# Spreading weight chunks, z rows and value tiles' loads, with identity products ahead of the first tile and the edge keys at a later tile

## The chip, the cores and the metric

The kernel runs on one core of one Trainium2 chip. The metric is the device time of one execution in microseconds (us), the median of several runs. A core has TensorE (PE, matrix products), VectorE (DVE), ScalarE (ACT), GpSimd (POOL) and SyncE (SP, which here only issues transfers); each works through its own instruction list in order, and semaphores order the engines among each other. Transfers between device memory and the on-chip buffer are issued by SP, ACT and POOL and carried by 16 DMA engines.

## What is computed

The reference is one layer on 2500 nodes with 1024 features: layer norm, a graph aggregation, an attention-like mix whose result is the value projection, and a feed-forward with ternary weights and rounded activations.

```python
xn = layernorm(x)
gnn = segment_sum((xn @ W)[src] * edge_w[:, None], dst, 2500)   # 42500 edges
q, k, v = xn @ Wq.T + bq, xn @ Wk.T + bk, xn @ Wv.T + bv
q, k = q / norm(q), k / norm(k)          # norms over the whole array
s = sum(phi(q) * phi(k), over the map)   # phi: exp of a product with mix weights
x = x + gnn + s * v / s
y = layernorm(x)
x = x + bitlinear(silu(bitlinear(y, w_gate)) * bitlinear(y, w_up), w_down)
```

`bitlinear` rounds each row of the input to 8-bit integers and the weights to -1, 0, 1.

## The kernel before, in words

The nodes are 20 tiles of 125 rows (`TILES`, `ROWS`), handled in 10 pairs (`HALF`), the two of a pair in buffers 0 and 1. In each product of single-precision data both factors are split into a high and a low part, and three matmuls give the product (`product3`, lines 374 to 376). ACT makes the high part, DVE subtracts it to get the low part, so each operand passes ACT, then DVE, then PE.

**First Gram pass** (PE lines 1522 to 1552). For each tile n: DVE computes row statistics (`row_sums`) and normalises (`normalise`, signals `s_xn`); PE turns the tile by eight transposes (line 1530); ACT copies the high part into a ring of three slots (`high_of_rows`), DVE the low part (`low_of_rows`, `s_lo`), and PE adds the tile's Gram products (lines 1515 to 1517, `s_gm`). ACT also brings the transposed tile out of PSUM and writes it to memory (`transposed_rows`, `write_transposed`; four buffers). At tile 4 PE transposes the edge keys and edge weights (line 1545), ACT copies them (line 808) and writes them as rows to memory (line 812, `s_kout`); at tile 5 the bias rows follow. The keys are computed by DVE in `edge_keys`, called ahead of tile 4, from two index ramps that POOL writes with `iota` (line 693) right after the identity. POOL then copies the identity to bf16, clears `zeros`, and writes zeros over the dense edge matrices in strips, strip r after 4r tiles.

**Second Gram pass and maps.** From tile 20 on, DVE does one pair of edge columns (`edges`) after each low part; that needs the key rows, broadcast to all partitions by SP (`load_key_rows`, issued after `s_kout`, ahead of the loads of `raw`). The pairs are then scattered into the two dense matrices by POOL until about 941 us.

**Value stage ("stage 4").** The matrix WH/WL holds the value weights in columns turned block by block (`high_of_block`, `low_of_block`, `s_vl`). For each tile PE multiplies, DVE adds the bias and scales (`stage4_tile`, `s_z`), SP loads x, stores the sum as z and loads the next transposed tile (`load_tile`) in the order of its list: for pair h and buffer i, load of tile t + 2, then z's store, then the wait for that store, then x's load. ACT's `high_of_tile` waits for the load and for PE to be done with the buffer.

**Aggregation.** Five groups of four target tiles (`GROUPS`, `GT`); for each group all 20 source tiles are multiplied, m = g * 10 + h counting the pairs. SP loads blocks of the two dense matrices (`load_next_A`, lines 601 to 605), DVE adds the two (`sum_of_blocks`, line 1282), ACT and DVE split the block (AH, AL) and the source (SH, SL; `SH_first`, `SL_first` for m = 0), and PE adds the products into eight PSUM banks (`sources`). PE's signal `s_pe5[i]` lets ACT overwrite buffer i. The first group waits for the last z tile before its target tile 1 (`s_z[1]`). At a group's end DVE adds z (`zr`, `add_z`) and later normalises and rounds the rows. For group 0, SP loads all of `zr` (2 MB) after A's load 1.

**Chunks.** During group 0 the three feed-forward matrices are made ternary in 12 chunks of 128 rows: POOL loads a chunk (`load_chunk`, chunks 0 and 1 after both first `s_pe5`), DVE scales and rounds it (two steps), ACT copies it to bf16, DVE turns its blocks, POOL writes it in eight transfers (`store_halves`). `CHUNKS_AT` says how many fall to each pair: 0, 0, 1, 1, 2, 1, 2, 1, 2, 2. SP loads them back as `wT` in three parts at A's loads 12, 13 and 14.

## Time and profile before

| | us |
|---|---|
| three runs, median | 1673.24 |
| three runs, lowest and highest | 1671.74, 1677.58 |
| the profiled execution | 1673.33 |
| its span, first to last instruction | 1671.3 |
| PE busy | 1638.4 |
| DVE, ACT, POOL busy | 1115.9, 495.5, 640.8 |

The span is the profiled execution's own time without what lies around it, here 2.0 us. A row of a timeline begins with the start in us from the span's start and the duration in us, and an entry in brackets tells how long the engine had been idle before and what it was released by. The mean granted clock of PE is 0.999 of full speed.

### The profile page before, as it was taken

The page shows a single profiled execution, that of the slowest core. Times are in us where ns is not written, and L with a number is a line of the kernel's source. Part 1 is how long each engine was busy: PE and PEld are TensorE (multiplying, and loading weights), DVE is VectorE, ACT ScalarE, POOL GpSimd, SP SyncE. Part 2 cuts the span into 40 slices and gives each one's busy share as a digit, 9 for nine tenths or more (in the row PEclk, how much of TensorE's full clock was granted, in tenths as well). Part 3 has the DMA queues.
Part 4 walks back from the last instruction along what each step waited for, and adds up shares of the span by engine and source line. Part 5 has one row for each costly group of instructions (what it writes and reads, how often), then busy time and mean ns, then how long its engine had stood idle before and what let it go on. Part 6 is the DMA issues. An engine that isn't in the chain of part 4 may idle for free.

```text
span 1671.3 us, 22573 instructions
## 1 busy us (share of the span) xinstructions
PE 1638.4 (98%) x7876; PEld 1328.2 (79%) x7876; DVE 1115.9 (67%) x2568; ACT 495.5 (30%) x598; POOL 640.8 (38%) x497
## 2 busy tenths in 40 slices
PE   6999999999999999999999999999999999999998
PEld 5999999877777888887888877878877877787665
DVE  7876583667777766655555566787575674674886
ACT  4632311322111111122300024433333332332553
POOL 2011555777777777776688405620000000000000
PEclk9999999999999999999999999999999999999999
DMA  9999978665686665557866556655445345433554
GB/s 312 397 406 338 312 247 251 170 150 112 167 207 146 180 150 146 131 135 177 239 131 141 140 178 197 194 174 161 122 137 138 110 129 135 135 113 96 148 172 123
DMA packets 154688, 302.87 MB, mean 181 GB/s; under 512 B 61537, under 2 KB 92305, under 8 KB 154626
## 3 DMA queue, kind: packets, MB, share of 16 engines
q1 hardware_dynamic: 78382, 206.81, 39.5%
q0 software_dynamic: 66192, 62.07, 16.8%
q10 hardware_dynamic: 10052, 33.26, 6.5%
q8 instruction: 27, 0.44, 0.1%
q14 instruction: 35, 0.29, 0.1%
HBM read 202.88 MB, written 99.20 MB: 181 GB/s over the span
## 4 chain that ended last, share of the span: by engine, by line
PE 84%; DVE 8%; DMA 4%; issue 2%; ACT 1%; POOL 0%; SPq 0%; ACTq 0%; DVEq 0%
PE PS L374 21%; PE PS L375 21%; PE PS L376 21%; PE PS L1515 4%; PE PS L1517 4%; PE PS L1516 4%; PE PS L1749 4%; DMA Aside<-A_dense 3%; PE PS L1779 2%; PE PS L1579 2%; DVE stats L1316 1%; DVE SL L1289 1%; DVE zr L1310 1%; DVE AL L1291 1%; DVE stats L1053 1%
## 5 line engine op out<-in xcount | busy, mean ns | idle before, releaser
L721 POOL DMA_INDIRECT A_dense<-wtot,cell x333 | 537.9, 1615 | 219.5 <-DMA A_dense<-wtot,cell 125.0
L374 PE MATMUL PS<-SL,AH 125*125 125x512 f32 x784 | 308.4, 393 | 6.7 <-DVE AL L1291 6.2
L375 PE MATMUL PS<-SH,AL 125*125 125x512 f32 x784 | 309.6, 395 | 0.0
L376 PE MATMUL PS<-SH,AH 125*125 125x512 f32 x784 | 309.4, 395 | 0.0
L374 PE MATMUL PS<-WL,xtH 128*125 128x512 f32 x640 | 251.9, 394 | 3.2 <-DVE xtL L1178 3.2
L375 PE MATMUL PS<-WH,xtL 128*125 128x512 f32 x640 | 251.6, 393 | 0.0
L376 PE MATMUL PS<-WH,xtH 128*125 128x512 f32 x640 | 251.2, 393 | 0.0
L1289 DVE TENSOR_TENSOR SL<-S,SH 125x1024 fp32r<-125x1024 f32 x98 | 119.5, 1220 | 136.5 <-ACT SH L944 136.5
L944 ACT ACTIVATE SH<-S 125x1024 fp32r<-125x1024 f32 (+1 forms) x98 | 103.9, 1061 | 334.0 <-PE PS L376 334.0
L374 PEld LDWEIGHTS PS<-SL,AH 125*125 125x125 f32 x784 | 145.4, 185 | 47.2 <-DVE AL L1291 9.2
L375 PEld LDWEIGHTS PS<-SH,AL 125*125 125x125 f32 x784 | 145.7, 186 | 36.2
L376 PEld LDWEIGHTS PS<-SH,AH 125*125 125x125 f32 x784 | 145.1, 185 | 35.0
L386 DVE SCALAR_TENSOR_TENSOR junk<-keyrow,key,ewrow 128x256 bf16<-128x256 f32 x336 | 148.8, 480 | 1.2 <-DMA ewrow<-weight_rows 1.2
L374 PEld LDWEIGHTS PS<-WL,xtH 128*125 128x125 f32 x640 | 118.5, 185 | 33.1 <-DVE xtL L1178 4.1
L376 PEld LDWEIGHTS PS<-WH,xtH 128*125 128x125 f32 x640 | 118.6, 185 | 29.2
L375 PEld LDWEIGHTS PS<-WH,xtL 128*125 128x125 f32 x640 | 118.7, 185 | 28.8
L375 PE MATMUL PS<-TH,xtL 128*125 128x512 f32 x320 | 126.5, 395 | 0.0
L376 PE MATMUL PS<-TH,xtH 128*125 128x512 f32 x320 | 126.0, 394 | 0.0
L374 PE MATMUL PS<-TL,xtH 128*125 128x512 f32 x320 | 125.9, 393 | 0.0
L1178 DVE TENSOR_TENSOR xtL<-xt,xtH 128x1000 fp32r<-128x1000 f32 x60 | 71.5, 1191 | 78.7 <-ACT xtH L862 75.2
L862 ACT ACTIVATE xtH<-xt 128x1000 fp32r<-128x1000 f32 x60 | 62.0, 1033 | 188.9 <-DMA xt<-xnT 188.3
L705 POOL DMA_DIRECT2D A_dense<-zeros x40 | 46.1, 1153 | 139.9 <-PE PS L1517 78.4
(190 smaller groups left out, 2602.3 us busy)
## 6 DMA issues: line engine op xcount, KB each, us to landing
A_dense<-zeros POOLq DMA_DIRECT2D x40, 1280.0 KB
xt<-xnT SPq DMA_DIRECT2D x60, 500.0 KB
Araw<-A_dense SPq DMA_DIRECT2D x100, 250.0 KB, 2.7
Aside<-A_dense SPq DMA_DIRECT2D x100, 250.0 KB, 3.0
keyrow<-key_rows SPq DMA_DIRECT2D x42, 512.0 KB
ewrow<-weight_rows SPq DMA_DIRECT2D x42, 512.0 KB
xnT<-XT ACTq DMA_DIRECT2D x20, 500.0 KB, 9.7
zx<-in_x SPq DMA_DIRECT2D x20, 448.0 KB
```

What stands on the lines that cost most here:

```text
L374: nc.tensor.matmul(o, lh, rl, start=start, stop=False)
L375: nc.tensor.matmul(o, ll, rh, start=False, stop=False)
L376: return nc.tensor.matmul(o, lh, rh, start=False, stop=stop)
L386: nc.vector.scalar_tensor_tensor(junk[:, slot, 2 * c:2 * c + 2, :].rearrange("p a n -> p (a n)"), row, key[:, col], wrow, ALU.is_equal, AL ...
L721: pool.indirect_dma_start(cells[m], bass.IndirectOffsetOnAxis(cell[:, col:col + 1], 0), wtot[:, col:col + 1], None, compute_op=ALU.add).th ...
L944: nc.scalar.activation(sh, S[0:ROWS, bass.ds(s, 1), :].rearrange("p o n -> p (o n)"), ACT.Copy).then_inc(s_s[i], 1)
L1178: nc.vector.tensor_tensor(xtL[i][:, :, :], xt[:, i], xtH[i][:, :, :].bitcast(F32), ALU.subtract).then_inc(s_xtl[i], 1)
L1289: nc.vector.tensor_tensor(sl, S[0:ROWS, bass.ds(s, 1), :].rearrange("p o n -> p (o n)"), sh.bitcast(F32), ALU.subtract)
L1515: nc.tensor.matmul(o, hi[:, cols], rl, start=first and opens, stop=False, skip_group_check=True)
L1516: nc.tensor.matmul(o, lo[:, cols], rh, start=False, stop=False, skip_group_check=True)
L1517: last = nc.tensor.matmul(o, hi[:, cols], rh, start=False, stop=last_one, skip_group_check=True)
L1749: last = nc.tensor.matmul(PS[0:ROWS, 2 * i + c, :], rqT[:, i, k, 0:ROWS], up_blocks(c, k), start=k == 0, stop=k == KT - 1)
```

## The change

Six things change; none of them alters what is computed.

- Ahead of its first tile PE multiplies the identity by itself ten times (`WARM`), into a bank that is written anew later.
- POOL writes the two index ramps after the first zero strip, when tile 1 is normalised, and no longer right after the identity; the first zero strip waits for tile 0's normalisation.
- DVE's `edge_keys` moves from ahead of tile 4 to ahead of tile 12's statistics (after tiles 10 and 11 are normalised), and the keys' and biases' transposes and copies from tiles 4 and 5 to tiles 14 and 15 (`KEYS_TILE`).
- SP issues the loads of value tiles 2 and 3 right after the last value block's load.
- One chunk per pair: chunks 0 to 8 in pairs 1 to 9 of group 0, chunks 9 to 11 in pairs 7 to 9 of group 1, which is therefore written out and no longer part of the loop. z's rows are loaded by tile after A's loads 2 to 5, and the three parts of `wT` after A's loads 12, 15 and 23.
- In PE's first pair of the aggregation both sources are multiplied for three target tiles, then the wait for the last z tile follows, then the fourth target tile for both.

The diff, cut to its core:

```diff
+KEYS_TILE = 14
+WARM = 10
...
-CHUNKS_AT = (0, 0, 1, 1, 2, 1, 2, 1, 2, 2)
+CHUNK_OF = {(0, h): h - 1 for h in range(1, HALF)} | {(1, h): h + 2 for h in range(3 + GT, HALF)}
+WEIGHTS_AT = (HALF + 2, HALF + 5, 2 * HALF + 3)
...
         sp.wait_ge(s_vl, 2)
         load_v_rows(7)
+        for i in range(2):
+            sp.wait_ge(s_xth[i], 2 * HALF + 1)
+            sp.wait_ge(s_xtl[i], 2 * HALF + 1)
+            load_tile(2 + i, i)
...
-            if not isinstance(h, int) or t + 2 < TILES:
+            if 0 < h < HALF - 1:
                 load_tile(nxt, i)
-            elif i:
+            elif h and i:
                 load_next_A(0)
...
         wait_stage4(sp)
-        load_next_A(1)
-        split_rows(sp, zr[:, :, :], z_d[0:GN, :].rearrange("(t r) d -> r t d", r=ROWS), s_zin)
-        for hh in range(2, HALF + 2):
+        for hh in range(1, WEIGHTS_AT[-1] + 1):
             load_next_A(hh)
-        for f in range(3):
-            for i in range(2):
-                sp.wait_ge(s_fout[i], 128 * (2 * f + 2))
-            sp.dma_start(wT[:, f], wT_d[4 * f:4 * f + 4].rearrange("c p n -> p c n")).then_inc(s_wT, 16)
-            load_next_A(HALF + 2 + f)
-        with sp.Fori(HALF + 5, GROUPS * HALF - 1) as hh:
+            if 2 <= hh < 2 + GT:
+                d = hh - 2
+                split_rows(sp, zr[:, d, :], z_d[d * ROWS:(d + 1) * ROWS, :], s_zin)
+            if hh in WEIGHTS_AT:
+                f = WEIGHTS_AT.index(hh)
+                for i in range(2):
+                    sp.wait_ge(s_fout[i], 128 * (2 * f + 2))
+                sp.dma_start(wT[:, f], wT_d[4 * f:4 * f + 4].rearrange("c p n -> p c n")).then_inc(s_wT, 16)
+        with sp.Fori(WEIGHTS_AT[-1] + 1, GROUPS * HALF - 1) as hh:
             load_next_A(hh)
...
-        for t in (key, away):
-            pool.iota(t[:, :], [[0, ROWS_C // 2], [1, 2]], base=A_PITCH - 2, channel_multiplier=A_PITCH,
-                      allow_small_or_imprecise_dtypes=True).then_inc(s_fill, 1)
...
         pool.wait_ge(s_const, 8)
-        for r in range(STRIPS):
-            if r:
-                pool.wait_ge(s_gm, min(4 * r, TILES))
+        pool.wait_ge(s_xn, 1)
+        zero_strip(0, 0)
+        pool.wait_ge(s_xn, 2)
+        for t in (key, away):
+            pool.iota(t[:, :], [[0, ROWS_C // 2], [1, 2]], base=A_PITCH - 2, channel_multiplier=A_PITCH,
+                      allow_small_or_imprecise_dtypes=True).then_inc(s_fill, 1)
+        for r in range(1, STRIPS):
+            pool.wait_ge(s_gm, min(4 * r, TILES))
             zero_strip(0, r)
...
-            if n == 4:
+            if n == KEYS_TILE:
                 for q in range(2):
                     act.wait_ge(s_tr0, q + 2)
...
+        def high_beside_chunk(g, h):
+            high_of_pair(g, h)
+            if (g, h) in CHUNK_OF:
+                c = CHUNK_OF[g, h]
                 act.wait_ge(s_fr[c % 2], c // 2 + 1)
                 if c >= 2:
                     act.wait_ge(s_fT[c % 2], c // 2)
                 nc.scalar.activation(gqb[:, c % 2, :], gwb[:, c % 2, :], ACT.Identity, bias=neg_round[:, :]).then_inc(s_fq16[c % 2], 1)
...
             if a == 2:
                 low_of_rows(2)
+            if a == KEYS_TILE - 4:
                 edge_keys()
...
-            dve.wait_ge(s_zin, g * 32 + 32)
+            dve.wait_ge(s_zin, 32 * GT + g * 32)
...
+        def low_beside_chunk(g, h):
+            m = g * HALF + h
+            c = CHUNK_OF[g, h]
+            i, f = c % 2, c // 4
+            low_of_sources(2 * h, 0, m)
+            sum_of_blocks(1, m)
+            dve.wait_ge(s_gw[i], c // 2 * 16 + 16)
+            nc.vector.tensor_scalar(gwb[:, i, :], gwb[:, i, :], wq_sc[:, f:f + 1, 1], 1.0,
+                                    ALU.mult, ALU.min).then_inc(s_fm, 1)
+            dve.wait_ge(s_fm, c + 1)
+            nc.vector.tensor_scalar(gwb[:, i, :], gwb[:, i, :], -1.0, ROUND, ALU.max, ALU.add).then_inc(s_fr[i], 1)
+            low_of_sources(2 * h + 1, 1, m)
+            sum_of_blocks(0, m + 1)
+            dve.wait_ge(s_fq16[i], c // 2 + 1)
+            if c >= 2:
+                dve.wait_ge(s_fout[i], c // 2 * 128)
+            turn_blocks(gTb[:, i, :], gqb[:, i, :]).then_inc(s_fT[i], 1)
+
         for h in range(1, HALF):
...
+            low_beside_chunk(0, h)
...
+        group(1)
+        for h in range(3 + GT - 1, HALF):
+            if (1, h) in CHUNK_OF:
+                low_beside_chunk(1, h)
+            else:
+                low_of_pair(1, h)
+        with dve.Fori(2, GROUPS - 1) as g:
             group(g)
...
         pe.wait_ge(s_const, 6)
+        for n in range(WARM):
+            nc.tensor.matmul(PS[:, 0, 0:P], ident[:, :], ident[:, :], start=True, stop=True)
         pe.wait_ge(s_pad, 3)
...
-            if n == 4:
-                pe.wait_ge(s_xev[0], 3)
+            if n == KEYS_TILE:
+                pe.wait_ge(s_xev[0], n // 2 + 1)
...
-                    if d == 1:
-                        pe.wait_ge(s_z[1], HALF)
...
+        def first_sources(i, tiles):
+            sh, sl = (b[0:ROWS, :] for b in first_S[i])
+            for d in tiles:
+                rows = slice(d * ROWS, (d + 1) * ROWS)
+                for c in range(2):
+                    cols = slice(c * 512, (c + 1) * 512)
+                    last = product3(PS[0:ROWS, 2 * d + c, :], AH[i][0:ROWS, rows], AL[i][0:ROWS, rows],
+                                    sh[:, cols], sl[:, cols], i == 0, False)
+            return last
+
+        for i in range(2):
+            pe.wait_ge(s_lo5[i], 1)
+            first_sources(i, ORDER[:-1])
+        pe.wait_ge(s_z[1], HALF)
+        for i in range(2):
+            first_sources(i, ORDER[-1:]).then_inc(s_pe5[i], 1)
+        other_sources(0)
```

## Rows read from the trace of the kernel before

**Rows 1.** The page's first part: busy time, share of the span, instructions.
```profile
PE 1638.4 (98%) x7876; PEld 1328.2 (79%) x7876; DVE 1115.9 (67%) x2568; ACT 495.5 (30%) x598; POOL 640.8 (38%) x497
```

**Rows 2.** PE's waits over the span: us in total, times, longest us.
```profile
PE PS L374 <- DVE AL L1291: 6.2, 6, 2.1
...
PE PS L374 <- DVE xtL L1178: 3.2, 2, 2.4
...
PE PS L374 <- DVE zr L1310: 0.5, 1, 0.5
```

**Rows 3.** Timeline of the start, four engines: start us, duration us, instruction.
```profile
5.22 1.93 POOL L693 IOTA away<- 128x336 f32 x1
...
6.98 1.44 DVE L1065 TENSOR_SCALAR X<-X,mv,rstd 125x1024 f32<-125x1024 f32 x1
...
7.35 0.51 POOL L697 MEMSET zeros<- 128x512 f32 x1
...
8.68 1.90 PE L1530 MATMUL PS<-ident,X 125*128 125x125 f32 x8 [8.68 <-DVE X L1065]
...
11.05 0.81 DVE L1065 TENSOR_SCALAR X<-X,mv,rstd 125x1024 f32<-125x1024 f32 x1
...
14.71 1.02 PE L1530 MATMUL PS<-ident,X 125*128 125x125 f32 x8
...
17.47 1.53 DVE L1065 TENSOR_SCALAR X<-X,mv,rstd 125x1024 f32<-125x1024 f32 x2
...
20.55 0.50 DVE L1076 SCALAR_TENSOR_TENSOR key<-iedge 128x332 f32<-128x332 int32 x1
```

**Rows 4.** Key rows: ACT's issue, packets at 46 to 48 us, DVE's first edge pair.
```profile
35.22 0.58 ACTq L812 DMA_DIRECT2D key_rows<-kT_sb  x1
...
DMA packets 284, 0.74 MB, mean 368 GB/s; under 512 B 27, under 2 KB 111, under 8 KB 284
...
83.43 0.48 DVE L386 SCALAR_TENSOR_TENSOR junk<-keyrow,key,ewrow 128x256 bf16<-128x256 f32 x1
...
86.44 1.23 DVE L1070 TENSOR_TENSOR ring<-X,ring 125x1024 fp32r<-125x1024 f32 x1 [1.43 <-ACT ring L772]
```

**Rows 5.** Timeline of the value stage's first tiles, SP and DVE.
```profile
763.27 0.34 SPq L539 DMA_DIRECT2D xt<-xnT  x1
...
782.09 0.35 SPq L539 DMA_DIRECT2D xt<-xnT  x1
...
788.61 1.20 DVE L1178 TENSOR_TENSOR xtL<-xt,xtH 128x1000 fp32r<-128x1000 f32 x1 [7.69 <-ACT xtH L862]
```

**Rows 6.** Beginning of aggregation: timelines of PE, ACT, POOL; landing of chunk loads.
```profile
983.73 0.47 PE L374 MATMUL PS<-SL_first,AH 125*125 125x512 f32 x1 [1.01 <-DVE zx L1251]
...
985.47 1.06 ACT L944 ACTIVATE SH<-S 125x1024 fp32r<-125x1024 f32 x1 [9.33 <-PE PS L376]
...
990.99 1.06 ACT L944 ACTIVATE SH<-S 125x1024 fp32r<-125x1024 f32 x1 [3.95 <-PE PS L376]
...
991.61 1.19 POOL L743 DMA_DIRECT2D gwb<-in_L_ffn_w_gate  x2 [50.82 <-PE PS L376]
...
gwb<-in_L_ffn_w_gate POOLq DMA_DIRECT2D x2, 512.0 KB, 4.4
```

**Rows 7.** DVE's timeline; PE's waits in 990:1020, 1080:1100, 1120:1140, 1220:1240 us.
```profile
1011.66 0.68 DVE L1282 TENSOR_TENSOR Araw<-Araw,Aside 125x500 f32<-125x500 f32 x1 [6.66 <-DMA Aside<-A_dense]
...
PE PS L374 <- DVE AL L1291: 2.1, 1, 2.1
...
1086.27 0.75 DVE L1367 TENSOR_SCALAR gwb<-gwb,wq_sc 128x1024 f32<-128x1024 f32 x1 [4.55 <-DMA gwb<-in_L_ffn_w_down]
...
PE PS L374 <- DVE AL L1291: 1.7, 1, 1.7
...
PE PS L374 <- DVE AL L1291: 1.2, 1, 1.2
...
PE PS L374 <- DVE AL L1291: 0.3, 1, 0.3
```

More of the change, by code:

```diff
@@ L96 @@
 END_AT = 229368
-CHUNKS_AT = (0, 0, 1, 1, 2, 1, 2, 1, 2, 2)
-assert len(CHUNKS_AT) == HALF and sum(CHUNKS_AT) == 12
+CHUNK_OF = {(0, h): h - 1 for h in range(1, HALF)} | {(1, h): h + 2 for h in range(3 + GT, HALF)}
+assert sorted(CHUNK_OF.values()) == list(range(12))
+WEIGHTS_AT = (HALF + 2, HALF + 5, 2 * HALF + 3)
 def split_rows(eng, dst, src, sem):
@@ L966, in _ @@
         act.wait_ge(s_mm[1], 3 * HALF)
-        chunk = 0
-        for h in range(1, HALF):
-            high_of_pair(0, h)
-            for c in range(chunk, chunk + CHUNKS_AT[h]):
+        def high_beside_chunk(g, h):
+            high_of_pair(g, h)
+            if (g, h) in CHUNK_OF:
+                c = CHUNK_OF[g, h]
                 act.wait_ge(s_fr[c % 2], c // 2 + 1)
@@ L974, in _, with high_of_group @@
                 nc.scalar.activation(gqb[:, c % 2, :], gwb[:, c % 2, :], ACT.Identity, bias=neg_round[:, :]).then_inc(s_fq16[c % 2], 1)
-            chunk += CHUNKS_AT[h]
+        for h in range(1, HALF):
+            high_beside_chunk(0, h)
         def move_rows(g):
             return bass.ds(g * GN, GN)
-        with act.Fori(1, GROUPS) as g:
+        def high_of_group(g):
             high_of_pair(g, 0)
@@ L993, in _ @@
             split_rows(act, zr[:, :, :], z_d[move_rows(g), :].rearrange("(t r) d -> r t d", r=ROWS), s_zin)
+        high_of_group(1)
+        for h in range(3 + GT, HALF):
+            high_beside_chunk(1, h)
+        with act.Fori(2, GROUPS) as g:
+            high_of_group(g)
             with act.Fori(3 + GT, HALF) as h:
@@ L1685, in sources @@
             sh, sl = SH[0:ROWS, i, :], SL[0:ROWS, i, :]
-            if isinstance(m, int) and m == 0:
-                sh, sl = (b[0:ROWS, :] for b in first_S[i])
             for d in ORDER:
```

33 lines of the change are left out of this document (7 added, 26 removed).

## Prediction

> **What bounds the kernel now.** The first page says that TensorE (PE) is busy 98% of the span [rows 1], so a change can only win PE's few idle microseconds: 1671.3 less 1638.4 is 33, of which 8.7 lie ahead of the first transpose [rows 1, 3]; the rest is PE's waits and the tail behind its last product. I therefore read the list of PE's waits first, then the timeline around each. In the reader's eye it should fall into places: the start, where PE follows VectorE (DVE) tile by tile; one 2.4 us wait in the value stage, for the tile split at 788.61 [rows 2, 5]; 1.01 us where aggregation begins [rows 6]; and 2.1, 1.7 + 0.5 and 1.2 us in the first and second group of aggregation [rows 2, 7]. Between about 87 and 776 us PE has no wait at all, so what is won at the start is kept.
>
> **Start: constants and first tile.** In the kernel before, the copy to bf16 and the zero strip's memset stand behind two iotas of 1.95 us on GpSimd (POOL) and so run while DVE normalises tile 0, which takes 1.44 us; the next one takes 0.81 [rows 3]. With the iotas gone from there, both POOL steps end near 4.2 us and tile 0 takes 0.81: -0.63, on the path, since DVE is the engine that all others follow here. The iotas (3.9 us) now start when tile 1 is normalised, 11.05 + 0.81 = 11.9, less 0.6, and end near 15.2; the next normalisation starts at 17.47 less 0.6 [rows 3], so they don't meet, and the keys wait for them only much later. The Trainium skill, page "SBUF — State Buffer", section "Who interferes with whom", says that a VectorE instruction in its two-port mode and a GpSimd instruction exclude each other for the whole instruction, whichever began first; if the iota did overlap the normalisation, that rule would give back up to 1.9 us, and the rows leave 1.6 us between them.
>
> **Ten products of the identity.** They fit between 3.4 us (the identity is ready) and 7.8; bound from the rows: eight cold transposes take 1.90 [rows 3], so ten products of like shape some 2.4 us, at most twice that if a plain product costs double, still done by 8.2. No semaphore waits on them. They can only save time by letting tile 0 run with short matmuls (1.02 for eight transposes against 1.90). But PE then waits longer for DVE: its next work, tile 2, is normalised at 17.47 + 0.81 whatever PE does, and PE is done with tile 1 at 18.2 even now. Cost and gain: 0.
>
> **Edge keys from tile 2 to tile 10, their transposes from tile 4 to 14.** DVE loses 1.02 us (20.55 to 21.57) ahead of tile 4 and gets it back ahead of tile 10. In steady state DVE spends about as long for a pair of tiles as PE, so the key step shows as a new PE wait of 1.0 at tile 10. ScalarE's (ACT) copies, two DMA issues (the first 0.58, [rows 4]) and the bias rows' turn stall PE at tile 15 as they did at tile 5. I walked the three queues through all 20 tiles with the rows' durations and these semaphores: before, the last tile's Gram products end at 86.3 as in the trace; after, at 85.6. So the stage gives -0.65, the 0.63 of tile 0; bounds 0 (lead used up by slower landings) and -1.7 (the key step hidden at tile 10).
>
> What moves with it is SP's queue: the broadcast loads of the key rows wait for the key writes, and DVE's first edge pair (at 83.43 now) for them. Today the key writes are issued at 35.22 and their small packets are seen until about 47 [rows 4], i.e. 11 us. After, ACT issues near 71.5 to 72.5; the input tiles are loaded by then, so I take 7 us for landing, then 7 us for the first megabyte of rows: 86. An edge pair of 1.6 us must be over 1.15 us plus a little before PE needs the next split tile, which today is begun at 86.44 with 1.43 us of waiting before it and needed at 90.3 [rows 4]: the rows may be as late as 87. Cost 0, bounds 0 and +4 (11 us and 8 us instead).
>
> **Value tiles' loads.** Today SP loads tile 2 at 763.27 and tile 3 only at 782.09, behind the store of tile 0 [rows 5]; the latter makes PE wait 2.4. Both now go right after the eighth value block's load, at about 751 and 757. ACT's split of tile 2 still waits for PE to leave the buffer, so PE's 0.8 us ahead of tile 2 (xtL waits, 3.2 in all [rows 2]) stays; tile 3's split is ready by 782.2, before PE needs it at 787.4. Tile 4's load stays behind the store of tile 1 and was 1.8 us ahead of need, less than the 2.4 won; without tile 3's half megabyte in the queue the store lands earlier. -2.2, bounds -1.8 and -2.4.
>
> **First sources, three tiles of each, then the fourth.** The wait of 1.01 for the last z tile [rows 6] goes: PE has 36 products x 0.23 = 8.4 us to do first. But the buffer of source 0 is now released after both: 24 products take 5.54 (985.47 to 990.99, ACT's two starts, [rows 6]); from 978.5, both sources end at 989.7 and the first is released at 988.6 instead of 985.5. Three steps hang on this (SH on ACT, SL and AL on DVE, 3.0 us), so the next source is ready at 991.65: a new wait of 1.95.
>
> **One chunk per pair, from the first pair.** DVE now waits for chunk 0 in pair 1, between the splits of two sources. POOL still loads it only when both first sources are done: issue 991.61 today, 0.9 earlier after, landing 4.4 [rows 6], so 995.1 to 995.3. Then two steps of 0.7, SL 1.14, AL 0.6: 998.6, and PE is free at 991.65 + 5.57 = 997.2. A second new wait, 1.35, bounds 0 and +3. Queued behind that wait on DVE: the split of source 3, the next block sum and chunk 0's turn. So the beginning of aggregation costs 1.95 + 1.35 - 1.01 = +2.3.
>
> **z rows by tile, and chunks 9 to 11 in group 1.** The 2 MB of z went ahead of the next A blocks, and DVE waited 6.66 for one: PE 2.1 [rows 7]. Half a megabyte after each of four pairs has 5 us until the next A load: -2.05. Two chunks in the last pair made DVE wait 4.55 at 1086.27 and PE 1.7, then 0.5 for the sums of z [rows 2, 7]; with one chunk per 11.1 us pair both go: -2.2. In group 1 the wait of 1.2 falls to what the later groups show with no weights in the queue, 0.3 [rows 7]: the first weights' load now comes behind the A blocks. -0.85; bounds for the three -3.5 and -5.3.
>
> **Sum.** -0.65 + 0 + 0 - 2.2 + 2.3 - 2.05 - 2.2 - 0.85 = -5.65. Against the profiled execution, 1673.33, that is 1667.7; its time is within 0.1 of the median of the runs, 1673.24, from which 1667.6 follows. I write 1667.6.
>
> **Rivals.** (a) *The key rows come too late and PE stalls in the second Gram pass*: slower than before. For it: the DMA engines are fully busy there, the landing took 11 us in the rows. Against it: SP's queue holds nothing else at that time. PE loses each microsecond beyond 87; the sum is used up at a landing of 92.7, and at 98 the kernel is 5 slower, 1678. (b) *Chunk 0 or the released buffer costs more*, its load sharing the queues with A blocks: at the bound +3 instead of 1.35, and z's rows in the way once more by 1: 1670.3. (c) *The identity products pay*: The Trainium skill, page "TensorE: Matmul & The Clock Gate", Part 1, says the clock is full only for an engine that has been busy, which speaks for this. As a mechanism here: tile 0's 8 transposes and six slow products are over some 2.4 us earlier and this reaches the end: 1665.2. Against it, PE's wait for tile 2. (d) *The spreading doesn't do what it says*: A's wait at 1011.66 comes from something else (the ternary stores or the chunks), 2.05 stays: 1669.7.
>
> **Chances.** Forecast 0.55, (a) 0.12, most of it a stall of 1 to 4 us, only 0.05 as large as to end slower; (b) 0.15; (c) 0.08; (d) 0.10. About 0.3%, 5.0 us, is what a measurement of this kernel can tell from no change. Faster by more (below 1668.2): most of the forecast's case (0.47) and (c), 0.55. Within: the rest of it, (b), (d), most of (a), 0.40. Slower: 0.05. The unknown costs alone reach from 1664.0 (-1.7 at the start, chunk 0 in time) to 1672; the range is 1663.5 to 1672.5.
>
> **What would show it.** First normalisation 0.81, last first-pass product near 85.6; a wait of 1 us at tile 10; first edge pair near 86 with no PE wait behind it; no xtL wait near 787; two new AL waits, about 1.9 and 1.4, near 985; none of 2 us near 1007; none above 0.5 in the second group. A PE wait behind the first edge pairs, or more than 4 us in the first two pairs of aggregation, makes the prediction wrong.

## The result, and the profile after

The changed kernel takes 1668.48 us (median of 9 runs, 1666.82 to 1669.69); the kernel before took 1674.46 beside it (9 runs). The ratio is 0.9958, 95% interval 0.9948 to 0.9967: 0.42% faster, where 0.34% was forecast. The medians themselves differ by 6.0 us, the ratio stands for 7.0. The ratios of this document leave out a single run of 5816 us, of the kernel with the old order of PE's first sources. The profiled execution's span fell from 1671.3 to 1666.6 us.

The page's busy times, the answer to [rows 1], and then PE's waits over the span (us in total, times, longest us), the answer to [rows 2]:

```profile
PE 1643.1 (99%) x7896; PEld 1333.1 (80%) x7896; DVE 1115.9 (67%) x2568; ACT 487.1 (29%) x591; POOL 636.8 (38%) x497
...
PE PS L1543 <- DVE ring L1090: 5.5, 4, 2.3
PE PS L1552 <- POOL earlier L698: 3.4, 1, 3.4
PE PS L377 <- DVE AL L1312: 3.4, 6, 1.7
...
PE PS L377 <- DVE xtL L1199: 0.8, 1, 0.8
```

The waits for AL fell from 6.2 to 3.4 us and those for xtL from 3.2 to 0.8. PE's busy time rose by 4.7 us, most of it by 20 more matmuls (the ten products of the identity show as 20, 4.35 us together); further down there are also two stretches in which products run at half clock.

The start, answering [rows 3], from the timelines of PE, DVE and SP (start us, duration us, instruction, idle time before it):

```profile
3.38 4.35 PE L1552 MATMUL PS<-ident 128*128 128x128 f32 x20 [3.38 <-POOL earlier L698]
...
6.67 0.81 DVE L1085 TENSOR_SCALAR X<-X,mv,rstd 125x1024 f32<-125x1024 f32 x1
...
7.59 1.05 PE L1560 MATMUL PS<-ident,X 125*128 125x125 f32 x8
...
8.38 7.34 SPq L501 DMA_DIRECT2D brows<-in_L_mix_bq  x1
...
27.07 2.47 DVE L1073 BATCH_NORM_STATS2 stats<-X 125x6 f32<-125x512 f32 x4 [1.68 <-DMA X<-in_x]
...
31.01 0.65 PE L1543 MATMUL PS<-ring 125*128 125x512 f32 x1 [2.35 <-DVE ring L1090]
31.45 0.63 PE L1544 MATMUL PS<-ring 125*128 125x512 f32 x1
...
87.30 0.28 PE L1543 MATMUL PS<-ring 125*128 125x258 f32 x1
```

Tile 0 is normalised in 0.81 us, as forecast, and turned at full clock. But DVE then waits 1.68 us for pair 3 of x, PE 2.35 us at tile 4, and behind that wait nine products start 0.32 to 0.43 us apart instead of 0.17 to 0.23. The first product of 258 columns, my mark for "15 tiles done" (called the 258-column product from here on), stands at 87.30 against 86.48 before: the start is 0.82 us slower, not 0.65 faster. What follows can be told by a ledger. ACT's high part of a source (line 954, 98 times) is released by PE at the same place in both kernels, so the difference of its n-th starts, after less before, is how far PE is ahead:

| place | before | after | difference | step | forecast |
|---|---|---|---|---|---|
| 15 tiles done | 86.48 | 87.30 | +0.82 | +0.82 | -0.65 |
| value stage, its last product on PE | 978.14 | 976.62 | -1.52 | -2.34 | -2.2 |
| aggregation, 4th start | 1002.10 | 1002.94 | +0.84 | +2.36 | +2.3 |
| 7th start | 1021.10 | 1019.62 | -1.48 | -2.32 | -2.05 |
| 21st start | 1101.74 | 1097.51 | -4.23 | -2.75 | -2.2 |
| 39th start (about the end of group 1) | 1203.39 | 1198.85 | -4.54 | -0.31 | -0.85 |
| 98th start | 1533.94 | 1529.39 | -4.55 | 0 | 0 |

The first two places are starts on PE. The value stage's step is the 2.43 us wait that is gone; the row of the list above shows its one wait left, 0.8. The begin of aggregation, answering [rows 6], timelines of ACT, POOL, PE and DVE:

```profile
986.89 1.06 ACT L954 ACTIVATE SH<-S 125x1024 fp32r<-125x1024 f32 x1 [12.27 <-PE PS L379]
...
988.85 1.19 POOL L753 DMA_DIRECT2D gwb<-in_L_ffn_w_gate  x2 [53.67 <-PE PS L379]
...
989.93 0.50 PE L377 MATMUL PS<-SL,AH 125*125 125x512 f32 x1 [1.74 <-DVE AL L1312]
...
990.61 0.63 PE L379 MATMUL PS<-SH,AH 125*125 125x512 f32 x1
...
992.72 0.75 DVE L1389 TENSOR_SCALAR gwb<-gwb,wq_sc 128x1024 f32<-128x1024 f32 x1 [2.26 <-DMA gwb<-in_L_ffn_w_gate]
```

The wait for z is gone and 1.74 us for the late buffer is new, both as forecast. Behind it PE runs at half clock until about 993.7. DVE waits 2.26 us for chunk 0, but PE, slowed down, never feels it. And late in group 1, DVE (answering [rows 7]):

```profile
1172.44 0.68 DVE L1303 TENSOR_TENSOR Araw<-Araw,Aside 125x500 f32<-125x500 f32 x1 [4.84 <-DMA Aside<-A_dense]
1173.04 0.75 DVE L1389 TENSOR_SCALAR gwb<-gwb,wq_sc 128x1024 f32<-128x1024 f32 x1
1173.82 0.69 DVE L1392 TENSOR_SCALAR gwb<-gwb 128x1024 f32<-128x1024 f32 x1
1174.43 1.22 DVE L1310 TENSOR_TENSOR SL<-S,SH 125x1024 fp32r<-125x1024 f32 x1
1175.57 0.67 DVE L1312 TENSOR_TENSOR AL<-Araw,AH 125x500 fp32r<-125x500 f32 x1
```

An A block that came late, two steps of a chunk behind it, and only then the source's low part: PE waits 0.5 us here, at a place where before had no wait. Yet before had the same late block. ACT loads 2 MB of z rows in this group, in one piece, at 1164.75 us before and at 1159.20 after, and the A block issued 3 us behind it takes 9.7 us to land before and 9.9 after, where the blocks ahead of it took about 3. DVE before:

```profile
1177.99 0.68 DVE L1282 TENSOR_TENSOR Araw<-Araw,Aside 125x500 f32<-125x500 f32 x1 [4.83 <-DMA Aside<-A_dense]
1178.58 1.22 DVE L1289 TENSOR_TENSOR SL<-S,SH 125x1024 fp32r<-125x1024 f32 x1
```

There the low part stands right behind the late sum; the 1.4 us of chunk 9's two steps between them are what is new.

### The profile page after: what moved, and what is told of

It is laid out like the page before. It is cut to its first block, busy times and chain, and to the rows that moved or that the text cites. A ratio compares the mean times of both kernels' runs of the same rounds, so it can differ in the third digit from the quotient of the medians.

```text
span 1666.6 us, 22401 instructions
## 1 busy us (share of the span) xinstructions
PE 1643.1 (99%) x7896; PEld 1333.1 (80%) x7896; DVE 1115.9 (67%) x2568; ACT 487.1 (29%) x591; POOL 636.8 (38%) x497
## 4 chain that ended last, share of the span: by engine, by line
PE 85%; DVE 7%; DMA 5%; SPq 1%; issue 1%; ACT 1%; DVEq 0%; ACTq 0%
PE PS L377 21%; PE PS L378 21%; PE PS L379 21%; PE PS L1543 5%; PE PS L1545 5%; PE PS L1544 5%; PE PS L1794 4%; DMA Aside<-A_dense 3%; PE PS L1824 2%; PE PS L1609 2%; DVE SL L1310 1%; DVE stats L1337 1%; DVE zr L1331 1%; DVE AL L1312 1%; DMA z<-zx 1%
```

## The experiments

Twelve kernels, in three series of four. Each ratio is against before, from runs on the same chip; an interval reaches 0.12 to 0.22 points to each side, which is 2 to 4 us, so the profiles carry the finer readings. Each kernel has one profiled execution.

**Without the identity products.**

```diff
-WARM = 10
+WARM = 0
```

> The changed kernel without the ten products of the identity; all else stays. Theory (the products pay nothing, because the first tile's transposes are followed by waits for tiles 1 to 3 either way): time within 0.3 us of the changed kernel; tile 0's transposes take 1.9 us instead of 1.05, and the wait that follows is shorter by the same 0.85, so that tile 1's transposes start at the same offset; the half-clock products of 31 to 34.5 us stay. Rival (the identity products pay, since they bring full clock to the first tiles): slower by 1 to 2.5 us, with later transposes of tiles 1 to 3 and a first pass that ends later by as much.

Ratio 0.9960 (0.9948 to 0.9973), against 0.9958 with them: no cost and no gain in time. Its trace, PE:

```profile
8.28 1.90 PE L1560 MATMUL PS<-ident,X 125*128 125x125 f32 x8 [8.28 <-DVE X L1085]
10.61 0.80 PE L1543 MATMUL PS<-ring 125*128 125x512 f32 x1 [0.42 <-DVE ring L1090]
...
30.54 0.50 PE L1543 MATMUL PS<-ring 125*128 125x512 f32 x1 [1.58 <-DVE ring L1090]
```

The transposes take 1.90, as in [rows 3], the first eight products behind them are slow, and the 30.54 product is at full clock: the half-clock stretch has gone back to tile 0, where DVE is waited for anyway. My theory that the stretch behind tile 4 would stay was wrong; that the products gain nothing was right. The 258-column product comes at 86.04. DVE's wait for pair 3 is 0.92 here, though nothing was changed for it. Near 988 this kernel has the same wait of 1.74 us as the changed one, but no slow products behind it; there 0.36 us for chunk 0 shows instead.

**The bias rows' loads behind pair 4's.**

```diff
-        for i, v in enumerate((bq, bk)):
-            sp.dma_start(brows[0:KT, i, :], ...)
         for p in range(3, NP):
             sp.wait_ge(s_st, 2 * (p - 2))
             load_pair(p)
+            if p == 4:
+                for i, v in enumerate((bq, bk)):
+                    sp.dma_start(brows[0:KT, i, :], ...)
```

> The changed kernel with the two loads of the bias rows issued on SP behind the load of pair 4 of x, not ahead of pair 3's. In the changed kernel SP spent 7.34 us on them (8.38 to 15.7), pair 3's load was issued at 16.42, DVE waited 1.68 us for it, PE waited 2.35 us at tile 4 (31.01) and its products ran at half clock until about 34.5. Theory (the late pair 3 is what ate the start's gain): no wait of DVE for pair 3, none over 0.5 us of PE near 31, no products of 0.63 us there, and a first pass that ends 1.5 to 3.5 us earlier: faster than the changed kernel by that. Rival (the wait near 31 comes from the DVE's own order of work, not from the load): pair 3 lands earlier, PE's wait stays over 1.5 us, time within 0.5 us of the changed kernel.

Ratio 0.9961 (0.9947 to 0.9975). DVE's wait for pair 3 and PE's at tile 4 are gone, as the theory said; yet a half-clock stretch is there all the same, now from about 20.4 us, and the 258-column product comes at 86.33: 0.97 us earlier than in the changed kernel, not 1.5 to 3.5. The long issue only moved: SP needs 3.76 and 2.70 us for pair 3's two transfers in place of 7.34 for the bias rows.

**The old order of PE's first sources.**

```diff
-        for i in range(2):
-            pe.wait_ge(s_lo5[i], 1)
-            first_sources(i, ORDER[:-1])
-        pe.wait_ge(s_z[1], HALF)
-        for i in range(2):
-            first_sources(i, ORDER[-1:]).then_inc(s_pe5[i], 1)
+        pe.wait_ge(s_lo5[0], 1)
+        first_sources(0, ORDER[:-1])
+        pe.wait_ge(s_z[1], HALF)
+        first_sources(0, ORDER[-1:]).then_inc(s_pe5[0], 1)
+        pe.wait_ge(s_lo5[1], 1)
+        first_sources(1, ORDER).then_inc(s_pe5[1], 1)
```

> The changed kernel with the old order of TensorE's first products of the aggregation: all four tiles of source 0, a wait for the last z tile ahead of its tile 1, then all of source 1. Theory (moving that wait behind source 1 made source 0's buffer free later, so DVE's SL and AL of the next pair are late by the 1.74 us wait near 990): PE waits about 1.0 us for z near 986, the 1.74 us wait near 990 goes, and the products of 0.63 us that followed it (990 to 993.4, some 1.6 us lost) go too, unless chunk 0, whose wait of DVE is now bare, brings a PE wait of 1 to 2.4 us at the next source. Sum between -2.3 and +0.8 us against the changed kernel. Rival (chunk 0, not the buffer, makes that wait): the 1.74 us wait stays and 1.0 us is added.

Ratio 0.9969 (0.9956 to 0.9982): 1.8 us above the changed kernel by the ratios, with intervals that overlap; I had expected -2.3 to +0.8. PE and DVE:

```profile
981.93 0.49 PE L377 MATMUL PS<-SL_first,AH 125*125 125x512 f32 x1 [0.93 <-DVE zx L1272]
...
993.67 0.76 DVE L1389 TENSOR_SCALAR gwb<-gwb,wq_sc 128x1024 f32<-128x1024 f32 x1 [6.42 <-DMA gwb<-in_L_ffn_w_gate]
...
996.94 0.50 PE L377 MATMUL PS<-SL,AH 125*125 125x512 f32 x1 [2.26 <-DVE AL L1312]
```

The 1.74 us wait is gone: it did come from the late buffer. The z wait is back, 0.93, and chunk 0, no longer covered, costs 2.26. So the forecast's two new waits are two mechanisms, and this kernel shows the second without the first. At ACT's 4th start it is 0.1 us ahead of the changed kernel; it falls behind in group 1, where it waits 2.26 us near 1178 and the changed one 0.5.

**New order: one tile of source 1 ahead of the z wait, source 3's low part ahead of chunk 0.**

```diff
         pe.wait_ge(s_lo5[0], 1)
         first_sources(0, ORDER[:-1])
+        pe.wait_ge(s_lo5[1], 1)
+        first_sources(1, ORDER[:1])
         pe.wait_ge(s_z[1], HALF)
         first_sources(0, ORDER[-1:]).then_inc(s_pe5[0], 1)
+        first_sources(1, ORDER[1:]).then_inc(s_pe5[1], 1)
...
+            if m == 1:
+                low_of_sources(2 * h + 1, 1, m)
+                sum_of_blocks(0, m + 1)
             dve.wait_ge(s_gw[i], c // 2 * 16 + 16)
...
-            low_of_sources(2 * h + 1, 1, m)
-            sum_of_blocks(0, m + 1)
+            if m != 1:
+                low_of_sources(2 * h + 1, 1, m)
+                sum_of_blocks(0, m + 1)
```

> The changed kernel with two edits at the start of the aggregation: TensorE does source 0's tiles 0, 2, 3, then source 1's tile 0, then waits for z, does source 0's tile 1 and frees its buffer, and then source 1's tiles 2, 3, 1; and DVE does the low part and the sum of source 3 before the steps of chunk 0. Theory (the 1.74 us wait near 990 comes from the late release of source 0's buffer, and the slow products behind it from that wait): source 0 is freed 1.9 us or more earlier, neither the 1.01 us z wait nor the 1.74 us wait is there, no products over 0.6 us between 985 and 1000, and chunk 0's load is covered: 2.0 to 3.3 us faster than the changed kernel. Rival (the slow products belong to the time or the load on the chip and not to the wait): the products of 0.63 us stay, and only 1.2 to 1.7 us is gained.

Ratio 0.9940 (0.9921 to 0.9960), 1665.29 us. The stretch 990:1000 (busy us and instructions of PE, PEld, DVE, ACT, POOL, then granted clock, DMA share, GB/s) of the changed kernel and then of this one:

```profile
990.00:1000.00 10.00, 10.00 (x37) 7.88 (x38) 6.91 (x9) 3.35 (x4) 2.61 (x6) 0.83 0.75 244
```

```profile
980.00:990.00 10.00, 10.00 (x45) 7.99 (x44) 6.25 (x7) 2.13 (x3) 0.00 (x0) 1.00 0.22 59
990.00:1000.00 10.00, 10.00 (x45) 8.01 (x44) 7.14 (x9) 3.62 (x5) 3.47 (x7) 1.00 0.74 248
```

"Busy" is 10.00 in all of them, and only the counts and the clock tell that the first did 37 products and the others 45. From the value stage's last product to ACT's 4th start this kernel takes 22.7 us, the changed one 26.3 and before 24.0: 3.6 us are gained at this place. The profile's gain (1664.3 against 1666.6) is smaller, mainly by the 1.38 us that PE waits at 800.62 for a load of the value stage.

**The identity products alone, in the kernel before.**

```diff
         pe.wait_ge(s_const, 6)
+        for n in range(10):
+            nc.tensor.matmul(PS[:, 0, 0:P], ident[:, :], ident[:, :], start=True, stop=True)
         pe.wait_ge(s_pad, 3)
```

> The kernel before with the ten products of the identity ahead of tile 0, and nothing else of the change. In the looks so far each of the four kernels with these products had its cold stretch (products of 0.63 us, some 3.5 us long) between 20 and 35 us, and the two without had it at tile 0 (11 to 13.5 us), where 1.3 us waits for DVE follow anyway. Theory (the products only move the cold stretch from covered to bare work): tile 0's products at full clock, a stretch of 0.63 us products between 18 and 36 us, and the first product of 258 columns between 86.5 and 88.5 us against 86.48 of before: 0 to 2 us slower. Rival (they pay, as in the third rival of the forecast): no stretch behind tile 0 and the first product of 258 columns 0.5 to 1.5 us earlier than before's. Rival (they do nothing either way): within 0.3 us of 86.48.

Ratio 1.0006 (0.9993 to 1.0019). PE:

```profile
11.00 0.50 PE L1515 MATMUL PS<-ring 125*128 125x512 f32 x1 [1.43 <-DVE ring L1070]
...
20.70 0.79 PE L1515 MATMUL PS<-ring 125*128 125x512 f32 x1 [1.28 <-DVE ring L1070]
21.29 0.63 PE L1516 MATMUL PS<-ring 125*128 125x512 f32 x1
...
32.45 0.51 PE L1515 MATMUL PS<-ring 125*128 125x512 f32 x1 [2.10 <-DVE ring L1070]
```

The slow stretch is where the theory put it, and the 258-column product is at 88.87, outside the 86.5 to 88.5 expected and 2.39 us later than before's; 1.5 us of that stand already at tile 4 (32.45 against 30.92), where a late pair 3 makes PE wait 2.10, so the products' own share is not told. By time it is no change. The rival in which the products pay falls: the interval leaves them 1.2 us at most, where it had 2.4.

**The value tiles' loads alone, in the kernel before.**

```diff
         load_v_rows(7)
+        for i in range(2):
+            sp.wait_ge(s_xth[i], 2 * HALF + 1)
+            sp.wait_ge(s_xtl[i], 2 * HALF + 1)
+            load_tile(2 + i, i)
...
-            if not isinstance(h, int) or t + 2 < TILES:
+            if 0 < h < HALF - 1:
                 load_tile(nxt, i)
-            elif i:
+            elif h and i:
```

> The kernel before with the value tiles' loads of tiles 2 and 3 issued ahead of the loop, one tile later for the rest, and nothing else of the change. Theory (the 2.43 us wait near 790 is for a load behind stores and x loads in SP's queue): that wait goes, no other over 0.5 us comes in the value stage but one at tile 1 of 0.80, and the kernel is 2.0 to 2.5 us faster than before. Rival (the wait is given back at the z wait or later in the stage): a new wait between 795 and 985 us and less than 1 us of gain. Since one look at a variant of the changed kernel had 1.38 us at 800 for the same kind of load, a wait of that size may show here too: then the gain is about 1 us.

Ratio 0.9982 (0.9967 to 0.9997): 3.0 us, interval 0.5 to 5.5, forecast 2.2. In the value stage only the 0.80 us wait is left, and from the 258-column product to the stage's last one 2.7 us are saved. Its trace teaches something else: at 1015 us, where before waits 2.05, and at 1089, where it waits 1.71, this kernel, with the same code there, waits 0 and 1.0. Its span of 1665.7 is thus 5.6 below before's, of which the edit gave 2.7; and this execution, at 1667.72, was the fastest of the twelve, whose median is 1672.86.

**z rows in one piece.**

```diff
         for hh in range(1, WEIGHTS_AT[-1] + 1):
             load_next_A(hh)
-            if 2 <= hh < 2 + GT:
-                d = hh - 2
-                split_rows(sp, zr[:, d, :], z_d[d * ROWS:(d + 1) * ROWS, :], s_zin)
+            if hh == 1:
+                split_rows(sp, zr[:, :, :], z_d[0:GN, :]...., s_zin)
...
-            dve.wait_ge(s_zin, 32 * GT + g * 32)
+            dve.wait_ge(s_zin, 32 + g * 32)
```

> The changed kernel with the z rows of group 0 loaded in one piece behind the first of the A loads, as before, and nothing else. Theory (z rows spread give 2.05 us): a PE wait of 1.5 to 2.5 us comes back between 1000 and 1025 us, and the kernel is 1.5 to 2.5 us slower than the changed one. Rival (the wait near 1015 was from two chunks falling on one pair, not from the z rows): no wait over 0.5 us there, time within 0.5 us of the changed kernel.

Ratio 0.9997 (0.9983 to 1.0011), against 0.9958: 6.5 us slower than the changed kernel, three times the forecast's term. The trace has the same: from ACT's 4th to 7th start 23.24 us, and 16.68 in the changed kernel. DVE and PE:

```profile
1012.84 0.68 DVE L1302 TENSOR_TENSOR Araw<-Araw,Aside 125x500 f32<-125x500 f32 x1 [7.65 <-DMA Aside<-A_dense]
1013.43 1.24 DVE L419 STREAM_TRANSPOSE gTb<-gqb 128x1024 bf16<-128x1024 bf16 x1
...
1016.42 0.79 PE L377 MATMUL PS<-SL,AH 125*125 125x512 f32 x1 [3.61 <-DVE AL L1311]
```

The mechanism is the forecast's (2 MB ahead of an A block, [rows 7]), but the chunks now begin in pair 1, so a chunk's turn stands between the late block and the split; PE waits 3.61 and then runs at half clock (233 products in 1000:1060 instead of 261). Spreading z is what makes early chunks affordable. Group 1, whose z rows still come in one piece, pays the same way at chunk 9.

**Three cures together: new order, no identity products, bias rows later.**

```diff
-WARM = 10
+WARM = 0
...
(the new order and the bias rows' loads as above)
```

> The changed kernel without the ten identity products, with the bias rows' loads behind pair 4's, and with the start of the aggregation as in the run with the new order (source 1's first tile ahead of the z wait, source 3's low part ahead of chunk 0). Theory (the three stalls are independent): first product of 258 columns at 84.5 to 85.6 us, no half-clock products but at tile 0, no PE wait between 980 and 1060, span 1660 to 1662.5 us, 0.55 to 0.7% faster than before. Rival (the starts are bounded by the loads of x and by DVE, so that two cures give what one gives): first product of 258 columns at 85.8 to 86.4 us and a span of 1662.5 to 1664.

Ratio 0.9937 (0.9915 to 0.9958), 1665.63 us, but a span of 1665.8, above what either case gave; the profiled execution was the slowest of its six (1667.71, the others 1663.01 to 1666.47). The trace says why: pair 3 landed late though the bias rows were out of its way, and a late A block came in group 1.

```profile
9.14 5.96 SPq L109 DMA_DIRECT2D X<-in_x  x1
15.14 2.39 SPq L110 DMA_DIRECT2D X<-in_x  x1
...
31.54 0.80 PE L1548 MATMUL PS<-ring 125*128 125x512 f32 x1 [2.94 <-DVE ring L1091]
...
1172.14 0.68 DVE L1304 TENSOR_TENSOR Araw<-Araw,Aside 125x500 f32<-125x500 f32 x1 [6.77 <-DMA Aside<-A_dense]
...
1175.99 0.50 PE L377 MATMUL PS<-SL,AH 125*125 125x512 f32 x1 [2.44 <-DVE AL L1313]
```

**The edge keys at their old tile.**

```diff
-KEYS_TILE = 14
+KEYS_TILE = 4
...
-            if a == KEYS_TILE - 4:
+            if a == 2:
                 edge_keys()
...
-            if n in (5, KEYS_TILE + 2, KEYS_TILE + 3):
+            if n in (5, 6, 7):
```

> The changed kernel with the edge keys back at their old place (DVE's three key operations behind pair 2, their transposes at tile 4), everything else as changed. In the changed kernel DVE came to pair 3 of x 1.7 us earlier than before, and waited 1.68 us for its load: the time of the keys turned into a wait. Theory (the move of the keys is worth nothing at the start, since the load of pair 3 sets DVE's pace): DVE's wait of 1.0 to 2.2 us for X is gone or under 0.6, PE's wait at tile 4 stays within 0.5 us of the 2.35 us of the changed kernel, the first product of 258 columns stays between 87.0 and 87.8 us. Rival (the keys' move is what moved the start, by taking cover from the load): the first product of 258 columns 0.5 us or more earlier than 87.3. Rival (the move gains): it comes at 88 us or later.

Ratio 0.9972 (0.9958 to 0.9985), 2.3 us above the changed kernel's, with intervals that overlap. The 258-column product is at 87.28, as expected; DVE's wait for pair 3 fell only to 0.86 and PE's at tile 4 to 1.52, both outside what I had written. DVE began on pair 3 when its load was there, with the keys ahead of it (27.95) and without (27.07), so the key work fills a wait that is there anyway. The slow stretch was at tile 0 this time, identity products or not. That is why the two marks agree: tile 4's products start 0.87 us later than in the changed kernel (31.88), and that kernel then loses as much to its slow products. What the keys' move is worth alone, this pair does not tell.

**New order without the identity products.** Edit: `WARM = 0` on top of the new order.

> The changed kernel with the new order at the start of the aggregation and without the ten identity products; the bias rows' loads stay where they are. Theory (the two are independent): PE has no wait and no half-clock products between 980 and 1000 us, the first product of 258 columns comes at 86.0 to 87.2 us, and the time is 0.55 to 0.7% below before's. Rival (no gain from leaving the products out, as the timed rounds of the run without them hint): within 0.5 us of the run with the new order alone, that is 0.6% below before.

Ratio 0.9940 (0.9921 to 0.9959), 1664.12 us, span 1661.6. The 258-column product is at 85.52, better than the 86.0 to 87.2 expected; DVE began on pair 3 at 25.7; no wait and 88 products in 980:1000. The rival on the time holds: the ratio is that of the new order alone. At 50.72 PE waits 0.67 us: it fits the key step's wait at tile 10 that the forecast set at 1.0. Seven of the ten kernels with the keys' move show such a wait, 0.58 to 0.69; the changed kernel, late anyway, did not.

**The writes of zeros four tiles later.**

```diff
-        pool.wait_ge(s_xn, 1)
-        zero_strip(0, 0)
         pool.wait_ge(s_xn, 2)
...
-        for r in range(1, STRIPS):
-            pool.wait_ge(s_gm, min(4 * r, TILES))
+        for r in range(STRIPS):
+            pool.wait_ge(s_gm, min(4 * r + 4, TILES))
```

> As the run before it (new order, no identity products), and GpSimd's writes of zeros to the dense matrix (1280 KB each) come four tiles later each: the first at tile 4's product and not at 8.2 us, beside the loads of x pairs 3 and 4. Theory (the DMA engines are full from 0 to 60 us, and the first write of zeros is what pushes pair 3's landing to 27 us): SP's issues of pair 3 are shorter or earlier, DVE's wait for pair 3 goes, PE's waits at tiles 4 to 6 stay under 1 us, first product of 258 columns at 84 to 85.8 us: 0.5 to 2 us faster than the run before it. Rival (other loads, edges, mixing weights and rows, fill the engines until then): pair 3 lands within 0.7 us of 27 us and the first product of 258 columns stays at 86 us or later.

Ratio 0.9942 (0.9922 to 0.9961). SP's issue of the first bias row shrank to 3.59 us, DVE did not wait for pair 3, PE has no wait over 0.7 behind its first tile, and the 258-column product is at 85.71, inside the 84 to 85.8 expected, but no earlier than in the run before it, which had an early landing without this. By time it is nothing; whether the start is steadier, one profiled execution can't tell.

**Both loads out of the way.** Edit: the last one, and the bias rows behind pair 4.

> As the run with the zeros written later, and with the bias rows' loads behind pair 4's too. Theory (both stand ahead of pair 3 in time): first product of 258 columns 0 to 1 us earlier than in the run before it, none of PE's waits before 60 us over 1.3 us. Rival (one of them is enough, DVE and ACT set the pace then): within 0.3 us of the run before it.

Ratio 0.9940 (0.9921 to 0.9959), 1663.51 us, span 1660.8. The 258-column product is at 85.61, within 0.1 of the run before: the rival, DVE and ACT set the pace then. The five kernels with the new order (0.9937 to 0.9942) can't be told apart by time; each is about 10 us below before and 3 below the changed kernel. Each interval alone touches the changed kernel's (0.9948 to 0.9967); that all five ratios lie together below it, and the 22.7 us of the table below in every trace, are what speaks for the gain. They are the best found.

## Why the prediction was right, and where not

**The total** was -5.65; the ledger has -4.55, the timed ratio -7.0 (5.5 to 8.7), the medians -6.0: forecast and result agree within what these can tell. The terms do not agree so well, and part of the agreement is luck: the start lost 0.8 us where 0.65 was to be won, and at the begin of aggregation a stretch of slow products stood in for a wait that hardly came. The stages, in us, of all fourteen profiled executions (1 is the 258-column product, 2 the value stage's last product; 3 to 7 are ACT's 4th, 7th, 21st, 39th and 98th start):

| kernel | to 1 | 1 to 2 | 2 to 3 | 3 to 4 | 4 to 5 | 5 to 6 | 6 to 7 |
|---|---|---|---|---|---|---|---|
| before | 86.48 | 891.66 | 23.96 | 19.00 | 80.63 | 101.65 | 330.55 |
| before with products of the identity | 88.87 | 892.89 | 23.96 | 18.13 | 79.91 | 101.43 | 331.18 |
| before with value tiles' loads | 87.19 | 888.96 | 23.94 | 16.77 | 79.90 | 101.63 | 329.95 |
| changed | 87.30 | 889.32 | 26.32 | 16.68 | 77.89 | 101.34 | 330.54 |
| no identity products | 86.04 | 888.97 | 25.35 | 16.68 | 77.89 | 101.99 | 330.52 |
| bias rows later | 86.33 | 888.97 | 26.30 | 16.68 | 77.89 | 101.91 | 330.08 |
| old order | 87.46 | 888.96 | 26.39 | 16.68 | 77.89 | 103.12 | 329.98 |
| z in one piece | 87.45 | 888.96 | 25.31 | 23.24 | 77.89 | 102.91 | 330.29 |
| keys at their old tile | 87.28 | 888.97 | 26.30 | 16.68 | 77.89 | 102.40 | 330.30 |
| new order | 87.28 | 890.59 | 22.68 | 16.68 | 77.89 | 101.65 | 330.20 |
| three cures together | 89.03 | 888.96 | 22.69 | 16.99 | 77.89 | 103.01 | 329.98 |
| new order, no identity products | 85.52 | 888.96 | 22.68 | 16.68 | 77.89 | 102.58 | 330.04 |
| zeros later | 85.71 | 888.96 | 22.68 | 16.68 | 77.89 | 101.90 | 330.56 |
| zeros and bias rows later | 85.61 | 888.97 | 22.68 | 16.68 | 77.89 | 101.45 | 330.22 |

Some stages repeat to 0.01 us with the same code (77.89 in eleven kernels, 888.96 or 888.97 in ten, 22.68 or 22.69 in five); group 1 (5 to 6) takes 101.34 to 103.12 with the same code. Of the signs that the forecast named, the early end of the first pass and the wait at tile 10 did not show in the changed kernel, nor did the second AL wait near 985. By terms:

- **First normalisation, 0.81: right in size, and not enough.** All eleven kernels with the ramps moved had 0.81; before had 1.44 and the two other executions with its code at the start 1.26 and 0.83. The gain was therefore 0 to 0.6, not a fixed 0.63.
- **The start as a whole: -0.65 forecast, +0.82 found; the failed step.** The forecast put the lead that the keys' move gives DVE into the sum as kept, and named "lead used up by slower landings" only as its bound, 0, with a loss excluded. The landing was not slower: DVE began on pair 3 at 27.07, before at 27.00 (25.4 to 28.5 in the fourteen executions). DVE's lead turned into a wait of 1.68 for a load that came when it had always come, and PE's tile 4 started at 31.01 against 30.92 before, with the whole lead gone. The loss on top of that comes behind this wait, where PE runs at half clock: from tile 4 to the 258-column product the changed kernel needs 56.29 us, before 55.56. That a wait can bring slow products was in no term. The identity products, put at 0, belong to this step too. Of the seven kernels with them six had a slow stretch behind tile 0, on bare work; of the seven without them all had it on tile 0, where DVE is late anyway, and one (the three cures together) had another at its 2.94 us wait.

  Pair by pair the kernels with these products have the 258-column product 1.3 to 2.4 us later (87.30 and 86.04, 87.28 and 85.52, 88.87 and 86.48), but in each pair DVE's begin on pair 3 was later too (27.07 and 26.60, 27.84 and 25.72, 28.52 and 27.00), so what is the products' own is not separated. By time no cost is seen (0.9960 against 0.9958, 0.9940 against 0.9940, 1.0006 against 1). That they pay, my rival (c), is refuted; whether they cost 1 us is open.
- **Value tiles, -2.2: right** (-2.34 in the changed kernel's trace, -2.7 in ten others; 3.0 by time, with 0.5 to 5.5, for the edit alone).
- **Begin of aggregation, +2.3: right in sum by luck, half wrong in make-up.** The z wait's 1.01 is gone and the late buffer's wait is 1.74 for 1.95: six products between the buffer's release and the end of both sources take 1.3 us (986.89 to 988.19), the forecast had 1.1. The second wait, for chunk 0, was put at 1.35; without slow products to cover it, it was 0.36 and 0.32. The load was issued 0.7 us after the last of the first sources' products and not 1.0, and landed in 3.9 us and not 4.4. What brought the sum to +2.36 is the half clock behind the first wait, which no term had: the stage takes 26.3 us in the three kernels that have both, 25.3 in the two with the wait and without slow products, where the forecast's own mechanisms are alone and cost +1.4. With the old order chunk 0's wait is 2.26 instead. The new order, which removes both waits, takes 22.7 in all five kernels: 3.6 us less than the changed kernel and 1.3 less than before.
- **z rows and chunks, -2.05 and -2.2: signs right, sizes of one execution.** The waits taken from [rows 7] vary with the same code: 2.05, 1.18 and 0 at 1015 us, 1.71, 1.0 and 1.0 at 1089 us. By the stages z's term is -2.3, -1.5 and -0.1 against the three executions of the old schedule, the chunks' -2.7, -2.0 and -2.0. Against that, z in one piece under the new chunk schedule costs 6.5. The worth of an edit depended on the others: rival (d), that the spreading does nothing, is refuted by that run.
- **Group 1, -0.85: mis-sized, and on average of the wrong sign.** The wait of 1.24 fell to 0.16, but a new wait stands near 1176 in every kernel with the new schedule: 0.5, 1.1, 1.1, 2.3, 0.8, 2.1, 2.4, 1.4, 1.7, 0.8, 0.4. None of the three executions with the old schedule has it. The group takes 101.6 us in those three, 101.3 in the changed kernel and 102.2 on average of the eleven with the new one: a loss of 0.6. The changed kernel's own execution, with -0.31, is the shortest of the eleven, which is luck. The forecast saw the 2 MB of z ahead of an A block in group 0 and not in group 1, where it put three of the chunks.
- **Key rows, rival (a):** ACT issued them at 70.06, the first edge pair ran at 84.26, with no wait of PE. SP, which waits for both writes, went on 3.0 us later:

```profile
73.10 0.35 SPq L472 DMA_DIRECT2D keyrow<-key_rows  x1
```

The landing took at most that, and not the 7 us of the forecast or the 11 of [rows 4], so this rival was farther off than it looked.
- **The range.** Its lower end, 1664.0, is not what its bounds add up to: -1.7 at the start and chunk 0 in time give 1665.2, the other lower bounds 1664.8.

## What to carry to other kernels

When an edit takes work off an engine that others follow, look for the landing time of that engine's next input before counting the gain. When it puts work onto one, look at what stands ahead of that place in the transfers: chunk 9 went behind a block that had always been late. A wait read from one execution is one draw: where it ends with a transfer, the same code gave 0 to 2 us, so a sum of such waits needs several executions or a range. And moving a release later to remove one wait is paid at the next user of that buffer; doing just enough ahead of the wait (one tile of the other source) gets both.

## What the runs showed of the hardware

- **Half clock behind a wait, sometimes.** PE fell to half clock (starts of 512-column products 0.43 us apart and not 0.23) at or behind waits of 1.74 us (three kernels), 1.97, 2.18, 2.23, 2.35, 2.94 and 3.61. It did not behind the same 1.74 in two other kernels, nor behind 2.05, 2.10, 2.13, 2.26, 2.35, 2.43 and 2.44. In four kernels, all with the identity products, it fell at tile 2, where two waits of 1.3 us stand close together; in two more with these products the same two waits had no such fall. The Trainium skill, page "TensorE: Matmul & The Clock Gate", section "HAM oscillation — how this bites in real kernels", describes a kernel in which every wait for a transfer sets the clock back, with waits mostly longer than these; here it happened in some executions only. Such a fall cost 0.7 to 3 us more: 0.7 behind tile 4 and 1.0 near 990 in the changed kernel, 2 behind tile 4 with the three cures together (57.5 us from there to the 258-column product, before 55.6), about 3 with z in one piece (28 products fewer in 60 us, 6.5 us, of which 3.6 are the wait).
- **Warming up moved the slow stretch, it did not remove it.** With ten products ahead of tile 0, its transposes took 1.05 in place of 1.90, and a stretch at half clock followed at 11, 20 or 31 us, behind PE's waits for DVE.
- **POOL and DVE got in each other's way, either way round.** In before the normalisation at 6.98 took 1.44 beside POOL's cast of 0.28; in the kernel with the value loads alone the two rows are

```profile
6.88 0.83 DVE L1069 TENSOR_SCALAR X<-X,mv,rstd 125x1024 f32<-125x1024 f32 x1
```

```profile
7.13 0.73 POOL L700 CAST ident<-ident 128x128 bf16<-128x128 f32 x1
```

and there it was the cast that took long, and released PE's first transposes at 7.97. The Trainium skill, page "SBUF — State Buffer", section "Who interferes with whom", says that whichever issues first holds the pair of memory ports that the two engines share, and the other stands still. That only one of the two is slowed in each execution fits; who came first the rows don't tell, since in before DVE is the slow one though its row begins 0.14 us ahead of the cast's (7.12).
- **An issue can block a queue for 7 us.** The issue of one bias row (1024 elements) kept SP for 3.59 to 7.52 us at about 8 us; issued at 17 us it took 0.30. It is the moment and not the transfer: pair 3's load took 5.96, 3.76 or 2.10 when it stood there. In the kernel with the bias rows later the DMA engines' busy share is 1.05, that is full, from 8 to 16 us, where the issues are long, but it is 1.05 from 17 to 18 us too, where the issue is short; what makes the difference is not shown.
